# Moving the gate projections and two transposes to a later place in a GLA + MoE kernel on eight cores

## What is computed

```python
q = _l2norm(h @ Wq); k = _l2norm(h @ Wk); v = h @ Wv      # h = rmsnorm(x)
alpha = sigmoid(h @ Wg)                                    # one gate per key channel
def step(S, inp):                                          # over the 2048 tokens, per head
    a_t, k_t, v_t, q_t = inp
    S = a_t[..., None] * S + k_t[..., None] * v_t[..., None, :]
    o_t = einsum('bhkv,bhk->bhv', S, q_t)
    return (S, o_t)
x = x + o @ Wo
```

## Time and profile before

| | |
|---|---|
| median of 2 runs | 6748.03 us (6747.1 to 6748.97) |
| the profiled execution | 6750.15 us; span of its slowest core (core 4) 6748.6 us |
| spans of the 8 cores | 6668.5 to 6748.6 us |
| busy, core 4 | PE 54%, PEld 33%, DVE 39%, ACT 19%, POOL 7% |
| mean granted TensorE clock, core 4 | 0.664 of full speed |

### The profile page before, as it was taken

One profiled execution on the slowest core, in us unless ns is written; L12 is line 12 of the kernel. 1 busy time (PEld: TensorE's weight loads), 2 busy tenths in 40 slices (PEclk: granted clock), 3 DMA queues, 4 the chain that ended last, 5 costly groups with the idle time before them and its releaser, 6 DMA issues.

```text
span 6748.6 us, 80901 instructions; the slowest of 8 cores (6668.5 to 6748.6 us)
## 1 busy us (share of the span) xinstructions
PE 3641.6 (54%) x23312; PEld 2242.9 (33%) x23312; DVE 2630.5 (39%) x8166; ACT 1251.8 (19%) x4201; POOL 459.8 (7%) x796
## 2 busy tenths in 40 slices
PE   3555466555355536655545553766544555467553
PEld 2333245322233324532223332553212333255331
DVE  2444411354444441135544444113454444321455
ACT  2222211110222221111022222111102222101110
POOL 2000100000100010000010001000001000100000
PEclk8666588755666658875566665986556666687655
DMA  5000240143400024013340003202233000410223
GB/s 74 4 1 1 34 80 1 25 65 67 91 4 1 1 40 73 1 32 69 60 87 4 1 1 59 55 1 50 50 72 76 4 1 1 90 24 1 53 49 74
DMA packets 113925, 248.97 MB, mean 37 GB/s; under 512 B 12336, under 2 KB 12368, under 8 KB 113504
## 3 DMA queue, kind: packets, MB, share of 16 engines
q0 software_dynamic: 90464, 193.46, 16.9%
q1 hardware_dynamic: 23040, 50.34, 3.5%
HBM read 386.63 MB, written 16.78 MB: 60 GB/s over the span
## 4 chain that ended last, share of the span: by engine, by line
PE 41%; DVE 20%; DMA 14%; issue 14%; ACT 7%; POOL 2%; DVEq 1%; SPq 1%; ACTq 0%; another core or an unknown queue 0%; POOLq 0%
DMA SCb<-WA 5%; DMA WA<-f 4%; PE PA L382 4%; PE PB L382 3%; DVE STATE L688 2%; DMA WA<-w 2%; DVE SCb L640 2%; PE PDB L1042 2%; PE PC L1018 2%; PE PA L1018 2%; PE PA L795 2%; DVE SFf L683 2%; PE PB L795 2%; PE PG L1042 1%; PE PC L824 1%
## 5 line engine op out<-in xcount | busy, mean ns | idle before, releaser
L382 PE MATMUL PA<-YT,WA 128*128 128x256 bf16 x2048 | 317.5, 307 | 154.3 <-DVE YT L367 49.3
L382 PE MATMUL PB<-YT,WA 128*128 128x256 bf16 x2048 | 315.1, 305 | 71.6 <-ACT YT L393 42.7
L814 DVE TENSOR_TENSOR YT<-YT,PDB 128x256 bf16<-128x256 bf16 x96 | 40.5, 422 | 719.5 <-PE PDB L809 719.4
L688 DVE SCALAR_TENSOR_TENSOR STATE<-STATE,SFf 64x64 bf16<-64x64 bf16 x1024 | 287.5, 281 | 62.2 <-DVE SFf L683 1.8
L1049 DVE CAST WA<-PDB 64x512 bf16<-64x512 f32 x256 | 174.9, 683 | 340.9 <-PE PDB L1042 338.8
L448 POOL TENSOR_TENSOR YT<-YT,SCb 128x256 bf16<-128x256 bf16 x256 | 166.1, 668 | 1941.2 <-ACT SCb L561 1643.9
L382 PEld LDWEIGHTS PA<-YT,WA 128*128 128x128 bf16 x2048 | 207.2, 107 | 249.3 <-issue 209.4
L419 DVE TENSOR_SCALAR rows<-PS 16x256 f32<-16x256 f32 x32 | 11.9, 407 | 705.2 <-PE PS L410 705.2
L382 PEld LDWEIGHTS PB<-YT,WA 128*128 128x128 bf16 x2048 | 211.6, 108 | 161.6 <-issue 117.9
L263 POOL DMA_DIRECT2D WA<-f x128 | 68.2, 576 | 2457.3 <-DVE SCb L965 1455.0
L1042 PE MATMUL PDB<-WA,SCb 64*64 64x512 bf16 x256 | 160.5, 627 | 111.9 <-DMA WA<-f 102.8
(11 more groups left out here) (237 smaller groups left out, 8207.1 us busy)
## 6 DMA issues: line engine op xcount, KB each, us to landing
WA<-w POOLq DMA_DIRECT2D x64, 684.0 KB, 37.3
WA<-f POOLq DMA_DIRECT2D x128, 256.0 KB, 9.3
WA<-f POOLq DMA_DIRECT2D x16, 2048.0 KB, 21.5
SCb<-WA SPq DMA_DIRECT2D x256, 128.0 KB
WA<-w POOLq DMA_DIRECT2D x84, 256.0 KB, 51.1
XS<-x POOLq DMA_DIRECT2D x64, 256.0 KB, 7.1
y<-SFf SPq DMA_DIRECT2D x32, 512.0 KB
WA<-Wq POOLq DMA_DIRECT2D x32, 256.0 KB, 10.8
```

Source lines behind the costliest of these rows:

```text
L382: bld.emit("t", [lambda e, kc=kc, mc=mc, wn=wn, pt_=pt_, c0=c0: e.matmul(pt_[:, c0:c0 + 256], wsl(wn, kc, mc * 128, 128), YT[:, A_H + kc * ...
L688: e.scalar_tensor_tensor(STT_[p64(hh), doff + hh * 64:doff + (hh + 1) * 64], STT_[p64(hh), soff + hh * 64:soff + (hh + 1) * 64], SF[p64(hh ...
```

## The change

Two things are moved, and nothing is added or taken away. In the gate stage, the Wg projections of a pair (pair_proj) are issued at the top of that pair's pass, for pairs 1 to 3 thus behind gate_tail of the pair before. In the head loop, gla_tr(cc+2) is issued behind the output matmuls (L698, L701) of iteration cc, ahead of the ACT cast L706, where it stood at the top of the iteration. The U matmul of cc then stands ahead of gla_tr(cc+2), and takes the copies of its own chunk.

```diff
-                prsl = {}
-
-                def pair_proj(pr2):
-                    for mc in (2 * pr2, 2 * pr2 + 1):
+                for pr in range(NKC // 2):
+                    m0, m1 = 2 * pr, 2 * pr + 1
+                    prsl = {}
+                    for mc in (m0, m1):
                         prsl[mc] = proj_mm("Wg", mc)
                         gcols.append((F_COLS + mc * 24, reg(rSF, "COL%d" % mc)))
-
-                pair_proj(0)
-                for pr in range(NKC // 2):
-                    m0, m1 = 2 * pr, 2 * pr + 1
                     for mc in (m0, m1):
                         st_spevac(mc, *prsl[mc])
                     for st in (st_exp, st_ln, st_scan, st_cols, st_acexp, st_fksub,
                                st_fkexp, st_gkprep, st_gkexp, st_bsub, st_eqek):
                         for mc in (m0, m1):
                             st(mc)
-                    if pr + 1 < NKC // 2:
-                        pair_proj(pr + 1)
                     for mc in (m0, m1):
                         gate_tail(mc)
@@
                     for cc in range(NC_T):
-                        if cc + 2 < NC_T:
-                            trs[cc + 2] = gla_tr(cc + 2)
                         if cc + 1 < NC_T:
                             pregs[cc + 1] = gla_prep(cc + 1, trs[cc + 1])
@@
                         ], reads=[rvbd, rscm, rqg, rsS], writes=[slo])
+                        if cc + 2 < NC_T:
+                            trs[cc + 2] = gla_tr(cc + 2)
                         bld.emit("s", lambda e, hp=hp, cc=cc, g=g, poc0=poc0: e.copy(
```

## The result

| | us |
|---|---|
| before, median of 10 runs | 6733.1 |
| after, median of 11 runs | 6856.6 |
| ratio after / before | 1.0145 (95% interval 1.0111 to 1.0179) |
| profiled executions, before and after | 6750.15 and 6825.38 |

The change makes the kernel 1.45% slower, 98 us (75 to 121 by the interval); forecast were 90 us, 6838. In part of the executions the cores of one die show a lower granted clock and take longer: of the nine executions of after that count in the ratio, four have one die at 0.656 to 0.661 and take 6846 to 6866 us, while the five with both dies at 0.664 or more take 6796 to 6825 us. The two profiled executions differ by 75 us; the slowest core, which the views show, is core 4 before and core 2 after.

What follows compares the result with a forecast made beforehand. No engine is saturated; the head loop is bound by handover latency between engines. Loss 0.98 minus gain 0.28 us, times 128 loops, plus 0 for the gate stage, adds 90 us to 6748: 6838, range 6785 to 6880.

Steps and rivals of the forecast that it cites:

- The gate edit at 0: Gate stage: moving the Wg matmuls costs 0, as pairs 2 and 3 finish 3.9 us before their reader L456.
- The slow clock forecast for pair 2: Gate stage: pair 2's 16 Wg matmuls run at 0.50 clock, 3.88 instead of 2.23 us, off the path.
- The gain in front, 0.28 us: Head loop, iteration 0: without transposes ahead, chunk 1's L635 and L640 start earlier, by 0.20 to 0.36 us per loop.
- The loss, twice 0.49 us: Head loop, chunks 2 and 3: DVE waits 0.49 us each for the late L635, 0.98 us per loop.
- The sum of seven distances: Head loop: L643 to next L640 through transposes, ACT copies and expansion, 2.09 us, against 1.60 of DVE's own work.
- The sum: Head loop: 0.98 loss minus 0.28 gain, 0.70 us per loop, times 128 loops, 90 us slower.
- DVE's own pauses: Head loop: DVE sometimes pauses between two instructions; pauses falling into the new wait would lower the sum; size left uncounted.
- The forecast of the rows: Head loop: about 0.65 us TensorE idle per late L635; DVE idle before L640 up by some 125 us in all.
- That the copies come in time (6712 us): Rival, head loop: the new wait vanishes and only the gain of 0.28 us per loop is left; 6712 us; chance 0.07.
- That only part of the wait shows (6775): Rival, head loop: pauses and quicker handover halve the 0.98 us; 0.21 per loop, 27 us slower, 6775; chance 0.09.
- That the Wg pairs come onto the path: Rival, gate stage: L456 of pairs 1 to 3 waits for Wg; up to 186 us more, 7024; chance 0.04.
- That the gain in front fails (6873): Rival, head loop: no gain before chunk 1 and the full loss, 0.98 us per loop, 6873 us; chance 0.06.

Runs made afterwards that it cites:

- the kernel with four passes: The changed kernel (after), with the Wg matmuls of pairs 1 to 3 done four times into the same PSUM slot; ratio 1.0235 to before.
- transposes two matmuls earlier: Against the kernel with only the transposes moved: they stand behind the U matmul, ahead of the output matmuls; ratio 1.0025 to before, 17 us.
- in PE's wait: Against before: U matmul of cc and transposes of cc+2 moved between V's expansion and the score matmul of cc+1; ratio 0.9935, 44 us faster.
- DVE's wait filled as well: Kernel with U and transposes between expansion and scores, plus U scaling and state update of cc between cc+1's V and score maskings; ratio 0.9613, 6473.4 us.
- two passes: The changed kernel (after), with the Wg matmuls of pairs 1 to 3 done twice into the same PSUM slot; ratio 1.0128 to before.

## Why the prediction was right

A handover is, in what follows, the distance from the start of an instruction to the start of one on another engine that waits for it.

*The gate edit at 0.* Right. In after, L456 waits for PE only in the first pair of each tile (50.7 us over 16 places; 49.1 before), and alone the edit measures 0.9976. The distances from pair to pair are 8.62, 8.67 and 8.66 us. The slow clock forecast for pair 2 is there: in after its window (135.4 to 139.1 us) has a granted clock of 0.56, and pair 3's (144.1 to 148.1) of 0.50. Pair 1 is slow too (126.8 to 130.8, 0.50), which the forecast didn't name; it lay off the path as well. The rule from the Trainium skill, page "TensorE: Matmul & The Clock Gate", section "Loop structure matters more than you think", that waits between matmuls send the clock down, was borne out on the clock and did not matter to the time. Nor does the mean clock tell the time: the kernel with four passes has the best of all on its slowest core (0.694, after 0.661), since it keeps PE busy with more matmuls, and is the slowest of them.

*The gain in front, 0.28 us.* Right in size: 1.43 became 1.15 us, and the kernel that keeps it without the loss is faster by 44 us, where 36 were worked out.

*The loss, twice 0.49 us.* Right in mechanism and nearly in size. The sum of seven distances read from other places of the trace gave 2.09 us from L643 to the late L640; the run shows 2.06 (164.90 to 166.96). The terms that came out shorter are the first (L637 to L693, 0.39 for 0.41) and the one between the two copies (0.16 for 0.17); the handovers between engines (0.46, 0.40, 0.37) are the same. So the distance between two maskings grew from 2.14 to 2.59 and 2.60 us, by 0.46 and not 0.49. The bracket of 0.49 us in the rows of after is the idle time since the end of the instruction before, a little more than the delay: DVE also takes a few hundredths between two instructions without a wait.

*The sum.* 0.70 us per loop was worked out. With the measured terms it is 2 x 0.46 - 0.28 = 0.64 us, and the mean spacing of seven loops rose by 0.61 us. So two thirds of the missing 0.09 us are the chain, summed too long by 0.03 us each time; the rest may be DVE's own pauses falling into the new wait, which the forecast had named and left uncounted, but no run takes it apart. On 128 loops the miss is 12 us. The profiled executions (75 us) agree with the loops (78 us).

How much of each time lies in the head loop, the traces tell. The distances between the L604 (L598) of successive loops, 7 in each of 16 tiles, 112 on the slowest core of each profile, have these means:

| kernel | us per loop | against before, x 128 | by the ratio |
|---|---|---|---|
| before | 9.92 | | |
| gate edit alone | 9.91 | -1 us | -16 us |
| transposes alone | 10.52 | +77 us | +63 us |
| after | 10.53 | +78 us | +98 us |
| transposes two matmuls earlier | 10.08 | +21 us | +17 us |
| in PE's wait | 9.60 | -40 us | -44 us |
| DVE's wait filled as well | 7.79 | -272 us | -261 us |

The loop loses as much with the transposes alone as with both edits, and the gate edit alone changes neither the loop nor the distances from pair to pair, so it has no part in the loss. The ratios scatter about the loops by up to 20 us, each within its interval. For after, the five executions named with the result have a median of 6808 us, 75 us above that of before, as the loops give; the 20 us by which the ratio exceeds them come with the other four, at 6846 to 6866 us.

*The forecast of the rows.* PE's new idle time per late expansion was put at 0.65 us and is 0.71; DVE's idle time before the masking was to rise by some 125 us. With 29.3 and 58.3 us in the two groups of before it rose by 93: the forecast of that row forgot that the 0.20 us in front of chunk 1 vanish with the gain, 26 us over 128 loops. The groups by form of before:

```profile
L640 DVE TENSOR_TENSOR SCb<-PS,kbdm 128x128 bf16<-128x128 f32 x256 | 74.7, 292 | 29.3 <-PE PS L635 25.3
L640 DVE TENSOR_TENSOR SCb<-PG,kbdm 128x128 bf16<-128x128 f32 x256 | 74.7, 292 | 58.3 <-PE PG L635 54.2
```

*The rivals.* That the copies come in time (6712 us) fell with the first bracket: the handover took the same 0.40 us in its new place as at a head's start. That only part of the wait shows (6775) fell with it, since the 0.49 us are there in full for chunk 2 and for chunk 3. That the Wg pairs come onto the path needs more than twice their work. That the gain in front fails (6873) fell with the 1.15 us.

## What to carry to other kernels

In a loop bound by handovers between engines, look for the place where the engine of a prefetch waits anyway, and put the prefetch there: not at the top, where it delays what is needed now (0.28 us here), and not at the bottom, where its own round trip (1.50 us from the first transpose to the masking of V, 165.46 to 166.96) is longer than the work left to hide it. The price of a moved step can be summed from handovers of the same kind read elsewhere in the trace. And once a wait on one engine is filled, read the next engine's: the same idea applied to DVE added some 217 us to the first's 44.

The order of before hides one thing more. With two sets of buffers, transposes at the top of iteration cc overwrite the copies that U of the same iteration still has to read: in before U's matmul (L676, 172.03 on PE) starts behind the copies of chunk 2 (171.32 + 0.26) and reads these in place of its own chunk's:

```profile
172.03 0.26 PE L676 MATMUL PDB<-SCb 64*64 64x64 bf16 x2
```

A time alone doesn't show that; every place behind U, as in after and the last kernel here, avoids it.

## What was not expected of the hardware

How fast the same 16 Wg matmuls ran depended on what PE did before them. Alone after idle time they took 3.88 us at a granted clock of 0.50. In the kernel with four passes, behind a pair that had kept PE busy since 126.78, all 64 of pair 2 took 9.3 us at 1.00, at 2.4 GHz from the first one.

With two passes the added work was cheap only in pair 2: 32 matmuls in 4.6 us (135.03 to 139.63, clock 1.00), where the single pass of after takes 3.6. In pair 1 the first 16 took 3.90 us at 0.50 and the next 16 2.37 us at 0.92, and pair 3 took 6.0 us at 0.72, against 3.9 us for the single pass in each. Even so none of this reached the time, because the reader came later still. Pair 1 also shows what stays open: it stands behind the same work in the kernels with two and with four passes, and ran its first matmuls at 0.50 in the one and at 1.00 in the other; no run here tells why.
